# Second feed-forward of a four-layer transformer: two stages of 11 weight steps, one per batch, become one stage of 22 steps, with the first batch's layer norm placed beside the second batch's first products

## The reference, cut to what matters

```python
gate = einsum('bsh,ih->bsi', x, Wg) * ag        # Wg, Wu: 1376 x 512
up   = einsum('bsh,ih->bsi', x, Wu) * au
h    = silu(gate) * up
out  = einsum('bsi,hi->bsh', h, Wd) * ad        # Wd: 512 x 1376
x    = layernorm(x + out)                       # no learned scale, over the 512 features
```

## Time and profile before

| what | value |
|---|---|
| median of 3 runs | 2195.33 us (2194.84 to 2196.17) |
| the profiled execution's own time | 2195.61 us |
| its span in the trace | 2193.5 us |
| PE busy | 1997.3 us, 91% of the span |
| DVE busy | 1109.3 us, 51% |
| ACT busy | 777.9 us, 35% |
| POOL busy | 741.3 us, 34% |
| the two stages that change | about 1218.7 to 1449.9 us of the span |

### The profile page before, as it was taken

How to read it: one execution, slowest core, us unless ns; L and a number is a source line. 1 busy time by engine, 2 the same in 40 slices (tenths; PEclk the granted TensorE clock), 3 DMA queues, 4 the chain that set the end, 5 groups by cost and what they waited for, 6 DMA issues and landing times.

```text
span 2193.5 us, 28280 instructions
## 1 busy us (share of the span) xinstructions
PE 1997.3 (91%) x10566; PEld 1259.8 (57%) x10566; DVE 1109.3 (51%) x2019; ACT 777.9 (35%) x1649; POOL 741.3 (34%) x1199
## 2 busy tenths in 40 slices
PE   5999976999999999999998897969999788999887
PEld 3545434777777777777776685834444444544333
DVE  4666445555555555555554414135555345565344
ACT  1565422433333333333332322313555202565311
POOL 2454304433343434334331433312444102343200
PEclk9899977999999999999999898989999889999899
DMA  7323000101010100101000521143333006111100
GB/s 190 43 38 94 2 19 0 49 1 49 1 49 1 49 13 37 49 1 49 1 30 0 192 87 58 44 55 38 58 63 99 9 0 74 33 43 41 38 20 19
DMA packets 45338, 95.02 MB, mean 43 GB/s; under 512 B 7594, under 2 KB 35626, under 8 KB 41898
## 3 DMA queue, kind: packets, MB, share of 16 engines
q1 hardware_dynamic: 42610, 90.86, 16.3%
q10 hardware_dynamic: 2592, 2.36, 0.8%
HBM read 62.20 MB, written 2.10 MB: 29 GB/s over the span
## 4 chain that ended last, share of the span: by engine, by line
PE 81%; DVE 10%; issue 3%; ACT 2%; DMA 2%; POOL 1%; POOLq 0%; ACTq 0%; SPq 0%; DVEq 0%
PE PS L1296 10%; PE PS L1365 8%; PE PS L1348 6%; PE PS L1321 6%; PE PS L1700 5%; PE PS L538 5%; PE PS L435 5%; PE PS L516 4%; PE PS L482 4%; PE PS L563 4%; PE PS L1333 3%; PE PS L1307 3%; PE PS L1711 3%; PE PS L1676 3%; PE PS L450 2%
## 5 line engine op out<-in xcount | busy, mean ns | idle before, releaser
L956 ACT ACTIVATE PB<-PS 128x512 f32<-128x512 f32 x480 | 281.0, 599 | 240.2 <-PE PS L516 237.2
L732 DVE TENSOR_REDUCE NM<-PS 128x2 f32<-128x1024 f32 x192 | 209.2, 1091 | 182.4 <-PE PS L484 181.0
L861 POOL TENSOR_SCALAR_AFFINE_SELECT PB<-PB 128x256 f32<-128x256 f32 (+1 forms) x480 | 174.2, 367 | 322.0 <-ACT PB L956 316.0
L1494 ACT COPY PRT<-PS 128x512 f32<-128x512 f32 (+3 forms) x256 | 108.8, 425 | 417.4 <-PE PS L1333 413.0
L482 PE MATMUL PS<-KQ 96*128 96x512 bf16 (+3 forms) x768 | 187.7, 309 | 31.1 <-DMA KQ<-LOW 16.0
L1454 DVE TENSOR_REDUCE NX<-PS 128x1 f32<-128x512 f32 (+3 forms) x256 | 124.0, 490 | 171.3 <-PE PS L1322 169.4
L1613 POOL TENSOR_SCALAR PR<-PR,RCP 128x512 f32<-128x512 f32 (+3 forms) x256 | 135.8, 536 | 200.8 <-DVE RCP L1442 194.5
L516 PE MATMUL PS<-KQ 99*128 99x512 bf16 (+3 forms) x768 | 183.1, 304 | 5.6 <-DMA KQ<-NMT 2.5
L1321 PE MATMUL PS<-kT,qT 128*128 128x512 f32 (+3 forms) x512 | 184.0, 441 | 4.2 <-ACT PR L1560 4.0
L274 POOL TENSOR_TENSOR rstd<-ve,halfneg 128x1 f32<-128x1 f32 x64 | 44.1, 689 | 369.3 <-DVE ve L250 369.3
L435 PE MATMUL PS<-XTT,WA 128*128 128x512 f32 x288 | 148.9, 627 | 13.2 <-DVE ident_masks_b L2075 11.7
(11 more groups left out here) (257 smaller groups left out, 3966.1 us busy)
## 6 DMA issues: line engine op xcount, KB each, us to landing
KQ<-HI SPq DMA_DIRECT2D x90, 128.0 KB, 3.9
KQ<-MID SPq DMA_DIRECT2D x72, 128.0 KB, 4.6
WB<-f_w SPq DMA_DIRECT2D x12, 768.0 KB, 4.4
WB<-w1o SPq DMA_DIRECT2D x8, 1024.0 KB, 8.0
WC<-f_w SPq DMA_DIRECT2D x10, 768.0 KB, 4.5
WB<-w1a SPq DMA_DIRECT2D x8, 768.0 KB, 4.4
WB<-w1b SPq DMA_DIRECT2D x8, 768.0 KB, 5.9
WA<-w SPq DMA_DIRECT2D x6, 1024.0 KB, 7.5
```

The lines of the kernel that those rows point to most:

```text
L732: x = dve.tensor_reduce(nm[:, h:h + 2, i], PS[:, b:b + 2, 0:(i + 1) * P], AX.X, ALU.max, negate=True)
L861: pool.affine_select(blocks, blocks, [[0, count], [1, P]], ALU.is_ge, 0.0, base=0, channel_multiplier=-1).then_inc(s16["probs_ready"].sem, 1)
L956: act.activation(PB[:, n % PBS, :], PS[:, 4 + n % 2, :], ACT.Exp, scale=self.scale)\
```

## The change

The two stages become one, with M = 22 steps. Steps 0 to 10 are batch 0, steps 11 to 21 batch 1; the same weight tiles are loaded a second time for the second batch, as before. `XH2` and `XL2` get room for both batches. `H1` and `AD` move into free columns of `WB`. The split of x is made chunk by chunk (cast c, subtract c) instead of four casts and then four subtractions; that of batch 1 is done by DVE behind steps 2 to 5. The tail of batch 0 is spread over steps 11 to 14 by hand. The tail of batch 1 stands at the end of the stage, as before. SP asks for `AGU` and `AD` ahead of the two biases of a2.

```diff
+        H1 = WB[:, 3072:4096].rearrange("p (s n) -> p s n", s=2)
+        AD = WB[:, 4096:4608]
...
+            def slot_free(self, eng, t):
+                if t >= 2:
+                    eng.wait_ge(self.s_x.sem, self.s_x.at(t - 1))
+                elif self.before:
+                    eng.wait_ge(self.before.s_x.sem, self.before.s_x.at(NT - 1 + t))
...
+            def down(self, pe, m):
+                pe.wait_ge(f1["h_lo"].sem, m + 1)
+                for t in range(NT):
+                    if m == M1:
+                        pe.wait_ge(self.tails[0].s_t.sem, self.tails[0].s_t.at(t + 1))
...
             def tensor(self, pe):
+                for m in range(M):
+                    self.gate_up(pe, m)
+                    if m == M1 + 1:
+                        for t in range(2):
+                            self.tails[0].turn(pe, t, PS[:, 4 + t, :])
+                    elif m == M1 + 2:
+                        for t in range(2, NT):
+                            self.tails[0].turn(pe, t, PS[:, 4 + t, :])
+                        self.down(pe, M1)
+                        self.down(pe, M1 + 1)
+                    elif m:
+                        self.down(pe, m - 1)
+                self.down(pe, M - 1)
+                self.tails[1].tensor(pe)
...
             def scalar(self, act):
...
+                for m in range(M):
...                 (wait for g(m), Silu of m)
+                    if m == M1 + 2:
+                        for t in range(2, NT):
+                            self.tails[0].take(act, t, PS[:, 4 + t, :])
+                    act.wait_ge(f1["h"].sem, m + 1)
                     if m >= 2:
+                        act.wait_ge(f1["down"].sem, m - 1)
+                    act.copy(HH[:, m % 2, :], H1[:, m % 2, :]).then_inc(f1["h_hi"].sem, 1)
+                    if m + 2 < M:
                         self.high(act, m + 2)
+                    if m == M1 + 1:
+                        for t in range(2):
+                            self.tails[0].take(act, t, PS[:, 4 + t, :])
+                self.tails[1].scalar(act)
...
+            def split_x(self, dve, b, c):
+                dve.tensor_copy(XH2[:, b, c, :], XTT[:, b, c, :]).then_inc(f1["x_hi"].sem, 1)
+                dve.wait_ge(f1["x_hi"].sem, NC * b + c + 1)
+                dve.tensor_tensor(XL2[:, b, c, :], XTT[:, b, c, :], XH2[:, b, c, :].bitcast(F32), ALU.subtract)\
+                   .then_inc(f1["x_lo"].sem, 1)
...
             def vector(self, dve, st):
                 for c in range(NC):
+                    self.split_x(dve, 0, c)
                 dve.wait_ge(f1["scales_loaded"].sem, 32)
+                one = self.tails[0]
+                for m in range(M):
+                    self.hidden(dve, m)
+                    if 2 <= m < 2 + NC:
+                        self.split_x(dve, 1, m - 2)
+                    if m == M1:
+                        one.mean(dve, st, 0, PS[:, 4, :])
+                        one.mean(dve, st, 1, PS[:, 5, :])
+                        one.finish(dve, 0)
+                    if m == M1 + 1:
+                        one.finish(dve, 1)
+                        one.mean(dve, st, 2, PS[:, 6, :])
+                        one.mean(dve, st, 3, PS[:, 7, :])
+                        one.finish(dve, 2)
+                        one.finish(dve, 3)
+                self.tails[1].vector(dve, st)
...
             def gpsimd(self, pool):
+                for m in range(M):
+                    pool.wait_ge(f1["w_hi"].sem, m + 1)
                     w = f1w[m % RING]
                     pool.tensor_tensor(WL[:, m % RING, :], w, WH[:, m % RING, :].bitcast(F32), ALU.subtract)\
                         .then_inc(f1["w_lo"].sem, 1)
+                    if m in (M1 + 2, M1 + 3):
+                        for t in range(2):
+                            self.tails[0].root(pool, 2 * (m - M1 - 2) + t)
+                self.tails[1].gpsimd(pool)
...
-        f1s = [Ffn1(b) for b in range(NB)]
+        f1s = [Ffn1()]
```

More of the change, by code:

```diff
@@ L236, in mean @@
                     else:
[L237 removed]
+                        dve.wait_ge(self.y_done[0].sem, self.y_done[1])
                     if self.biased:
@@ L1677, in gated @@
             return ins
+        M = NB * M1
         class Ffn1(Stage):
-            def __init__(self, b):
-                self.b, self.tail = b, Tail(b, y_done=(f1["down"], M1), mul=AD[:, :])
-            def tensor(self, pe):
[L1684 to L1714, removed]
@@ new lines, in build, with __init__, gate_up @@
+            b = 0
+            def __init__(self):
+                one = Tail(0, y_done=(f1["down"], M1), mul=AD)
+                self.tails = [one, Tail(1, y_done=(f1["down"], M), mul=AD, after=one)]
+            def gate_up(self, pe, m):
+                b = m // M1
+                high, low = WH[:, m % RING, :], WL[:, m % RING, :]
+                if m >= 2:
+                    pe.wait_ge(f1["h"].sem, m - 1)
+                pe.wait_ge(f1["w_hi"].sem, m + 1)
+                for kind, (w, x) in enumerate(((high, XH2), (high, XL2), (low, XH2))):
+                    if kind == 2:
+                        pe.wait_ge(f1["w_lo"].sem, m + 1)
+                    for bank, a in ((m % 2, 0), (2 + m % 2, 512)):
+                        for c in range(NC):
+                            if m % M1 == 0 and kind == 0 and not a:
+                                pe.wait_ge(f1["x_hi"].sem, NC * b + c + 1)
+                            if m % M1 == 0 and kind == 1 and not a:
+                                pe.wait_ge(f1["x_lo"].sem, NC * b + c + 1)
+                            ins = pe.matmul(PS[:, bank, :], w[:, a + c * P:a + (c + 1) * P], x[:, b, c, :],
+                                            start=(kind == 0 and c == 0), stop=(kind == 2 and c == NC - 1))
+                ins.then_inc(f1["gu_psum"].sem, 1)
@@ new lines, in down @@
+            def down(self, pe, m):
+                high, low = WH[:, m % RING, 1024:1536], WL[:, m % RING, 1024:1536]
+                pe.wait_ge(f1["h_lo"].sem, m + 1)
+                for t in range(NT):
+                    if m == M1:
+                        pe.wait_ge(self.tails[0].s_t.sem, self.tails[0].s_t.at(t + 1))
+                    rows = slice(t * P, (t + 1) * P)
+                    for i, (h, w) in enumerate(((HH, high), (HL, high), (HH, low))):
+                        x = pe.matmul(PS[:, 4 + t, :], h[:, m % 2, rows], w,
+                                      start=(m % M1 == 0 and i == 0), stop=(m % M1 == M1 - 1 and i == 2))
+                x.then_inc(f1["down"].sem, 1)
@@ L1726, in scalar @@
                 act.wait_ge(f1["scales_loaded"].sem, 32)
-                for m in range(M1):
-                    act.wait_ge(f1["gu_psum"].sem, f1["gu_psum"].at(m + 1))
+                for m in range(M):
+                    act.wait_ge(f1["gu_psum"].sem, m + 1)
                     if m >= 2:
-                        act.wait_ge(f1["h"].sem, f1["h"].at(m - 1))
-                    act.activation(SG[:, m % 2, :], PS[:, m % 2, :], ACT.Silu, scale=AGU[:, 0, m:m + 1])\
+                        act.wait_ge(f1["h"].sem, m - 1)
+                    act.activation(SG[:, m % 2, :], PS[:, m % 2, :], ACT.Silu, scale=AGU[:, 0, m % M1:m % M1 + 1])\
@@ new lines, in hidden @@
+            def hidden(self, dve, m):
+                dve.wait_ge(f1["silu"].sem, m + 1)
+                dve.scalar_tensor_tensor(H1[:, m % 2, :], PS[:, 2 + m % 2, :], AGU[:, 1, m % M1:m % M1 + 1],
+                                         SG[:, m % 2, :], ALU.mult, ALU.mult).then_inc(f1["h"].sem, 1)
+                dve.wait_ge(f1["h_hi"].sem, m + 1)
+                dve.tensor_tensor(HL[:, m % 2, :], H1[:, m % 2, :], HH[:, m % 2, :].bitcast(F32),
+                                  ALU.subtract).then_inc(f1["h_lo"].sem, 1)
@@ L2119, in _ @@
             until(a1)
-            Signal.batch = 0
             f1s[0].sync(sp)
-            Signal.batch = 1
-            f1s[1].sync(sp)
-            Signal.batch = 0
-            until(f1s[1])
+            until(f1s[0])
             a2.sync(sp, prefetch2)
```

69 lines of the change are left out of this document (20 added, 49 removed).

## The result

The changed kernel takes 2181.53 us (median of 4 runs, 2181.49 to 2183.09), against 2195.09 us for the kernel before (4 runs, 2194.26 to 2196.17): 13.6 us less, a ratio of 0.994 with a 95% interval of 0.9922 to 0.9957. Forecast were 2183.0 us and a range of 2178.5 to 2188.5. The profiled execution took 2181.49 us.

What follows compares the result with a forecast made beforehand. PE was taken as the bound (81% of the chain), with time won where it waits. Boundary gain 14.9 us minus start loss 2.5 gives 12.4; from 2195.6 that is 2183.2, median 2183.0 us, range 2178.5 to 2188.5.

Steps and rivals of the forecast that it cites:

- What DVE can do in time: Batch 0's tail: DVE adds of two SBUF inputs wait until POOL's `WL` ends; mean(0)'s gets in 0.06 us ahead.
- rival 1: Step 11: POOL's `WL`(13) goes before mean(0)'s add, making the whole chain 2.0 us later; 2185.0 us, chance 0.25.
- PE's gaps: Boundary of the batches: PE idles 1.6 us before turn(0), 1.6 before turn(1) and 1.9 before turn(2).
- g(14): Batch 1's fourth step on PE, 24 matmuls: starts 29.0 us behind Silu of step 11, at 1351.05 instead of 1365.98.
- The boundary: Between batch 0 and batch 1: one barrier, exposed tail and exposed start go; 14.9 us won.
- The turns: Batch 0's four tail turns, now among PE's work: 1.0 us each, 3.9 together, bounds 2.4 and 4.2.
- 0.8 us uncovered: One fall of PE's clock around turns 0 and 1, mostly hidden in g(13); 0.8 us added, bounds 0 and 3.4.
- Rival 3: From turns 0 and 1 on, the clock stays low; three steps at half clock lose 24.9 us, 2208 us; chance 0.02.
- The start: Start of the stage up to d(0): chunk-by-chunk casts wait for POOL's `WL`; 2.5 us lost.
- rival 2: Start of the stage: `XH` isn't blocked beside `WL`, gaining 1.4 us instead of losing 2.5; 2179.1 us, chance 0.12.
- The costs taken as nothing: Batch 1's split, late `high`(15) and `WL`(15), later weight loads, and moved `H1`, `AD`, `AGU`: no cost.
- Rival 4: Later stages: shifted transfers or clock phases return the boundary's gain as waits in a2; 2191 to 2195 us, chance 0.05.

Runs made afterwards that it cites:

- POOL first: Changed kernel, with mean(0) of batch 0 also waiting for the cast of `WH`(13), so `WL`(13) goes ahead of its add; 2184.04 us, single run.
- casts first: Changed kernel, with batch 0's split back to four casts, then four subtractions; 2186.07 us in a single run, 2183.85 us when run again.
- start gated: Changed kernel, with batch 0's four casts before its subtractions and POOL's `WL`(0) held until all four `XL` are done; 2174.44 us.
- two and four memsets: Changed kernel, with two or four DVE memsets of 128x512 added behind the stage's last tail; 2183.87 us with two, 2181.38 us with four.
- tail-exposed: Changed kernel's single stage, but batch 0's tail in one piece ahead of g(11), not spread over later steps; 2193.71 us, single run.

## Why the prediction was right, by its own steps

**What DVE can do in time** came out as told. The adds of mean(1) and mean(2) waited for `WL` (2.16 and 3.68 us), the one of mean(0) didn't, by the 0.06 us that had been read from the earlier trace rows. POOL first shows that rival 1 was right about its mechanism and its price: 1.95 us at turn(0), and as much at g(14) with the clock alike, with 2.0 forecast. The lead over POOL was thin but no accident: in all ten profiles with that order it was 0.04 to 0.07 us. PE's gaps of 1.6, 1.6 and 1.9 us were 1.55, 1.83 and 2.26.

**g(14)** was put at 29.0 us behind Silu of step 11, and started at 1351.99 - 1322.88 = 29.11. The boundary won 14.8 us, with 14.9 forecast. Part of that exactness is luck. The turns were taken at 1.0 us each; the first two took 0.66, at full clock, which only made the wait before turn(2) longer. And the clock was forecast to fall around turns 0 and 1, with 0.8 us uncovered. In the changed kernel it held there and fell at 1343.8, around turns 2 and 3, where nothing covers it: the 24 matmuls of d(11) and d(12) took 6.34 us instead of 5.60. The windows (length, busy PE, PEld, DVE, ACT, POOL, then clock, DMA share, GB/s) show it:

```profile
1334.00:1335.00 1.00, 0.00 (x0) 0.00 (x0) 1.00 (x2) 1.00 (x1) 0.00 (x0) 1.00 0.06 25
...
1344.00:1345.00 1.00, 0.97 (x5) 0.57 (x4) 1.00 (x2) 0.46 (x1) 0.00 (x0) 0.50 0.00 0
...
1347.00:1348.00 1.00, 1.00 (x5) 0.76 (x5) 0.00 (x0) 0.00 (x0) 0.00 (x0) 0.91 0.00 0
```

In casts first, start gated and the kernels with two and four memsets, whose order at the boundary is the same, it fell behind turn(0), where it was forecast. This row is from casts first, at turn(1) and the first products of g(13):

```profile
1335.00:1336.00 1.00, 1.00 (x5) 1.00 (x6) 0.96 (x2) 0.49 (x2) 0.91 (x1) 0.50 0.00 0
```

There all of it was hidden in the wait before turn(2), so the forecast's 0.8 us for an uncovered rest were not needed, nor 1.0 us for each of the last two turns (0.66), and the boundary took 41.7 us: 16.0 us won and not 14.9. The term of 0.8 us thus came out by a fall at another place. The place of the fall is worth 1.2 us, and it is not fixed by the order of the work. Rival 3, a clock that stays low, was not seen in any kernel that hides the tail: the longest low stretch at the boundary was under 7 us (13.7 us where the tail is exposed).

**The start** lost 1.56 us, with 2.5 forecast: here a term was mis-sized. Its mechanism is shown by casts first (back to 20.4) and by the cast of 3.65 us; rival 2, a cast that isn't blocked, is out. The size depends on when the clock rises behind 1228: 3.1 us behind PE's resumption in the changed kernel, 5.7 or 5.8 in the POOL-first and tail-exposed kernels, which lost 2.8. The bounds given, 1.5 to 3.1, held both; the middle was taken.

**The costs taken as nothing** were nothing. The split of batch 1 ran at 2.8 us of each step and delayed `WL` by 0.2; no matmul waited for the late `high`(15) or `WL`(15), nor for a weight load.

**Rival 4**, a gain given back behind the stage, was dismissed because a2's beginning is unchanged. In the changed kernel that was so (0.1 us). As a reason it was wrong: casts first gave back 6.1 us in stages of the same instructions, by the clock and not by waits in a2.

One part of the result was not in the sum at all: 0.75 us of the 13.8 lie ahead of the stage, where nothing was changed. The forecast of 12.4, with the start at its measured price, would have been 13.3; the measured boundary, start and rest of the stage give 13.2.

The upper end of the range, 2188.5, is more than its stated terms give: rival 1's 2185.0 with the clock's upper bound of 3.4 in place of 0.8 is 2187.6.

## What to carry to other kernels

Before placing a vector tail beside other work, list for each of its instructions whether it can run beside what GpSimd does then: here reading PSUM was free, and each add of two SBUF tiles or fast cast cost up to a whole 3.5 us subtraction. What paid most was to hold back the one that isn't urgent (one wait, 5.4 us) and to bring the whole tail between two of its instructions (2.5 us with the clock alike). Cutting its instruction in three gave 0.7. And judge an edit of 1 to 3 us by the stage's own stretches in the trace, since stages that it doesn't touch moved by 6 us; and look where the clock fell in each kernel before a difference of 1 us is put down to the edit.

## What the runs showed of the hardware that was not expected

- An idle PE between turns does not always lower its clock: with waits of 1.55 and 1.83 us around a turn of 0.66 it stayed at 1.00 in the changed kernel, and fell to 0.50 for 3.4 to 6.8 us in four others with the same order there.
- POOL and DVE take turns in the order of asking. `WL`(13), asked for at 1326.47 beside an add, took 4.01 us instead of 3.50, and then let the waiting add of mean(1) in before its own next instruction: the root that followed took 1.01 us instead of 0.55.
- The fast cast (0.42 us alone) is held off by a POOL memset, which reads nothing (1.21 us), while a two-input add beside one keeps 0.69.
